# Perceiver layer, cross-attention units: the mix of high and low context parts in 512-column matmuls, the sum moved to the normalisation, and the row maximum ahead of the last low third

## The reference, cut to what matters

```
xn  = layernorm(ctx)                 # 2 x 1024 x 256
ln  = layernorm(layernorm(x))        # 2 x 64 x 256
q   = ln @ Wq ;  k, v = split(concat(xn, ln) @ Wkv)
sim = rmsnorm(q) * scale @ rmsnorm(k)^T      # per head, 1088 keys
attn = softmax(sim)
x  += (attn @ v) @ Wout + bout
```

## Time and profile before

| | us |
|---|---|
| median of 3 runs | 232.57 (232.32 to 232.83) |
| profiled execution, its own time | 233.34 |
| its span, first to last instruction | 231.4 |
| TensorE busy | 220.6 |
| VectorE busy | 152.0 |
| ScalarE busy | 154.9 |
| GpSimd busy | 80.2 |

### The profile page before, as it was taken

The page is one execution under the profiler, slowest core; times in us unless marked ns, Lnnn a source line. Parts: engine busy times, 40 slices in busy tenths (PEclk is TensorE's granted clock), DMA queues, the critical chain, the costliest instruction groups (busy, mean ns, idle before and its releaser), DMA issues.

```text
span 231.4 us, 4188 instructions
## 1 busy us (share of the span) xinstructions
PE 220.6 (95%) x1446; PEld 190.8 (82%) x1446; DVE 152.0 (66%) x347; ACT 154.9 (67%) x340; POOL 80.2 (35%) x131
## 2 busy tenths in 40 slices
PE   7899999999989999999999999999999998999884
PEld 6556778887778888989888989899999987899773
DVE  2699899998778786776866755566766661303431
ACT  2868777979885968776676567778787755314151
POOL 5188897861592837445160500000000010000300
PEclk9999999999999999999999999999999999999999
DMA  6590134200000000000000899700000000000000
GB/s 184 151 317 32 47 122 175 68 25 0 23 0 3 1 4 0 0 3 0 0 0 3 256 428 328 177 3 0 0 4 0 1 3 0 0 3 0 0 3 23
DMA packets 11252, 13.80 MB, mean 60 GB/s; under 512 B 1592, under 2 KB 9952, under 8 KB 10976
## 3 DMA queue, kind: packets, MB, share of 16 engines
q1 hardware_dynamic: 10680, 11.97, 16.6%
q10 hardware_dynamic: 552, 1.58, 1.9%
HBM read 13.15 MB, written 0.13 MB: 57 GB/s over the span
## 4 chain that ended last, share of the span: by engine, by line
PE 65%; DVE 21%; ACT 5%; issue 4%; DMA 2%; POOL 2%; ACTq 0%; POOLq 0%; DVEq 0%
PE banks L1307 19%; PE banks L1157 14%; PE banks L1216 8%; PE banks L1248 8%; PE banks L1447 5%; DVE small L902 4%; DVE sk L914 4%; PE banks L1321 3%; DMA wraw<-in_L_xattn_Wkv 2%; PE banks L1250 2%; ACT knT L632 2%; PE banks L1370 2%; PE banks L1474 2%; DVE small L871 1%; DVE raw L865 1%
## 5 line engine op out<-in xcount | busy, mean ns | idle before, releaser
L937 DVE TENSOR_TENSOR ptl<-banks,pth 128x512 fp32r<-128x512 f32 (+1 forms) x48 | 26.8, 558 | 24.2 <-ACT pth L668 23.2
L1307 PE MATMUL banks<-xnh,pth 128*128 128x256 f32 x128 | 37.6, 294 | 0.1
L1307 PE MATMUL banks<-xnh,ptl 128*128 128x256 f32 x128 | 36.2, 283 | 0.0
L1307 PE MATMUL banks<-xnl,pth 128*128 128x256 f32 x128 | 36.2, 283 | 0.0
L515 POOL TENSOR_TENSOR small<-small 128x16 f32<-128x16 f32 x7 | 20.4, 2915 | 32.1 <-DVE small L909 32.1
L668 ACT ACTIVATE pth<-banks 128x512 fp32r<-128x512 f32 (+1 forms) x48 | 23.7, 495 | 10.6 <-PE banks L1157 9.5
L615 ACT ACTIVATE sk<-banks 128x512 f32<-128x512 f32 x36 | 20.7, 602 | 12.1 <-PE banks L1216 11.6
L902 DVE TENSOR_REDUCE small<-sk 128x8 f32<-128x512 f32 x36 | 23.6, 678 | 5.9 <-ACT sk L615 5.9
L914 DVE TENSOR_TENSOR sk<-banks,small 128x512 f32<-128x512 f32 x36 | 23.0, 680 | 6.6 <-POOL small L515 6.5
L495 POOL COPY sp<-sp 128x64 f32<-128x64 f32 x16 | 3.8, 238 | 62.8 <-ACT sp L649 62.7
L1157 PE MATMUL banks<-ident,sp 128*128 128x128 f32 x144 | 24.2, 279 | 1.1 <-ACT sp L649 1.1
(11 more groups left out here) (193 smaller groups left out, 478.0 us busy)
## 6 DMA issues: line engine op xcount, KB each, us to landing
knT<-in_L_attn_qkv_kernel SPq DMA_DIRECT2D x1, 3072.0 KB, 12.4
raw<-in_ctx SPq DMA_DIRECT2D x16, 128.0 KB, 2.3
knT<-in_L_xattn_Wq SPq DMA_DIRECT2D x1, 1024.0 KB, 6.8
wv<-in_L_xattn_Wkv ACTq DMA_DIRECT2D x1, 1024.0 KB, 4.9
wout_sb<-in_L_xattn_Wout SPq DMA_DIRECT2D x1, 1024.0 KB, 5.8
knT<-in_L_attn_out_kernel SPq DMA_DIRECT2D x1, 1024.0 KB, 15.2
wraw<-in_L_xattn_Wkv ACTq DMA_DIRECT2D x1, 512.0 KB, 5.0
wraw<-in_L_xattn_Wkv SPq DMA_DIRECT2D x1, 512.0 KB, 5.3
```

Of the source, the lines that this page charges most:

```text
L937: nc.vector.tensor_tensor(ptl[:, j0:j1, :], banks[:, t3_bank(u, c), 0:(j1 - j0) * P].rearrange("p (j r) -> p j r", j=j1 - j0), pth[:, j0:j ...
L1307: nc.tensor.matmul(banks[:, u_bank(u), 0:D], p_[:, j, :], x_, start=(j == 0 and i == 0), stop=False)
```

## The change

Units 8 to 14 become **wide** (`wide(u)`). `xnh` and `xnl` lie side by side in one array `xn2`, so that one matmul with 512 moving columns multiplies `pth` by both: high by high goes to the first half of the bank, high by low to the second. The matmul of `ptl` by `xnh` and those of the latents stay at 256 columns in the first half. The two halves are added where the mix is normalised: ScalarE scales the second half into `un` (`un_half`), then VectorE adds the first half, scaled, in one scalar_tensor_tensor (`mix_sum`), at the start of its work for the next unit.

The second half of the bank is now taken, so the transposed mix of a wide unit goes to the second half of bank 5 (`uT_bank`). That half holds the transposed feed-forward weights until L764 has copied them, so the wait for `w1T_ready` moves from ahead of the last logits third to ahead of `mix_transposed(u - 1)`.

From unit 7 on, `logits_max(u + 1)` is ahead of the low third `probs_low(u, 2)` on VectorE.

```diff
-        xnh = sb("xnh", [P, B * NT, D], F32R)
-        xnl = sb("xnl", [P, B * NT, D], F32R)
+        xn2 = sb("xn2", [P, B * NT, 2, D], F32R)
+        xnh = xn2[:, :, 0, :]
+        xnl = xn2[:, :, 1, :]
...
+        def wide(u):
+            return G <= u < UNITS - 1
+        def uT_bank(u):
+            return 5 if wide(u) else u_bank(u)
... (ScalarE, mix_out)
+                if wide(u):
+                    nc.scalar.activation(un[:, :], banks[:, u_bank(u), D:2 * D], ACT.Copy,
+                                         scale=rinv[:, u:u + 1]).then_inc(un_half, 1)
+                    return
... (ScalarE, mixT_out)
-                nc.scalar.activation(uT[:, :, :], banks[:, u_bank(u), D:2 * D].rearrange("p (c r) -> p c r", c=DC),
+                nc.scalar.activation(uT[:, :, :], banks[:, uT_bank(u), D:2 * D].rearrange("p (c r) -> p c r", c=DC),
... (VectorE)
+            def mix_sum(u):
+                dve.wait_ge(un_half, u - G + 1)
+                nc.vector.scalar_tensor_tensor(un[:, :], banks[:, u_bank(u), 0:D], rinv[:, u:u + 1], un[:, :], ALU.mult,
+                                               ALU.add).then_inc(un_ready, 1)
...
                 else:
+                    if wide(u - 1):
+                        mix_sum(u - 1)
                     probs_low(u, 0)
...
+                    if i + 1 >= ITEMS and u + 1 < UNITS:
+                        logits_max(u + 1)
                     probs_low(u, 2)
-                    if u + 1 < UNITS:
+                    if i + 1 < ITEMS:
                         logits_max(u + 1)
... (TensorE, mix)
+                        if wide(u):
+                            nc.tensor.matmul(banks[:, u_bank(u), :], pth[:, j, :],
+                                             xn2[:, b * NT + j, :, :].rearrange("p a d -> p (a d)"), start=(j == 0),
+                                             stop=False)
+                            nc.tensor.matmul(banks[:, u_bank(u), 0:D], ptl[:, j, :], xnh[:, b * NT + j, :], start=False,
+                                             stop=False)
+                            continue
... (TensorE, mix_transposed)
-                transposes(banks[:, u_bank(u), D:2 * D], lambda c: un[:, c * P:(c + 1) * P], DC).then_inc(ut_ps, 1)
+                transposes(banks[:, uT_bank(u), D:2 * D], lambda c: un[:, c * P:(c + 1) * P], DC).then_inc(ut_ps, 1)
... (TensorE, the loop over units)
                     if u >= G:
                         logits(u + 1, 0)
+                    if w1T_first < u <= w1T_first + len(w1T_blocks):
+                        pe.wait_ge(w1T_ready, u - w1T_first)
                     mix_transposed(u - 1)
...
                     probs_transposed(u, 2)
-                if w1T_first < u <= w1T_first + len(w1T_blocks):
-                    pe.wait_ge(w1T_ready, u - w1T_first)
                 logits(u + 1, 2)
                 mix(u)
```

More of the change, by code:

```diff
@@ L253, in perceiver_layer @@
         un_ready = sem("un_ready")
+        un_half = sem("un_half")
         ut_ps = sem("ut_ps")
```

## The result

The changed kernel takes 233.93 us (median of 6 runs, 233.60 to 234.08) against 232.53 for the kernel before (6 runs, 232.32 to 232.83). The ratio is 1.0055 with a 95% interval of 1.0042 to 1.0068: slower by 1.4 us, where 1.2 was forecast. The profiled execution took 233.99 us with a span of 232.2.

What follows compares the result with a forecast made beforehand. TensorE, busy for 95% of the span, was taken to bound the kernel. The terms 2.5 + 0.17 - 0.87 - 0.6 = +1.2 us, added to the 232.57 us median, gave 233.8 us, range 232.9 to 234.7.

Steps and rivals of the forecast that it cites:

- Part 3: Units 10 to 14: TensorE waits for ScalarE's weight copy before the mix transposes, 0.50 us each, a 2.5 us loss.
- Part 1: Starts of units 8 to 10: the earlier maximum closes TensorE's waits before the first transposes, a 0.87 us gain.
- Part 2: Wide units 8 to 14: 512-column matmuls save 10 ns in each of 56 context tiles, a 0.6 us gain.
- Part 4: Unit 9: TensorE waits 0.10 us for VectorE's added sum, 0.17 with refill, a loss of 0.2 us.
- refill: TensorE's queue restarting after a wait: four transposes take 0.42 us instead of 0.35, 0.07 us extra per wait.
- a weight load that idles 0.43 us on each copy: Units 10 to 14, sign of the forecast: the `un` transposes' weight load idles on L764's copy, some 2.1 us in all.
- the period: Sign of the forecast: the time per unit, 7.0 us before, rises to about 7.4.
- the copy cannot come earlier: ScalarE's weight copy hangs on TensorE's own transposes and the eviction between, so all of it shifts together.
- some 0.1 us of unit 10 would show: Claim that the weight copy's wait covers VectorE's sum in units 10 to 14; without it unit 10 would stall.
- TensorE makes up the wait: Rival, units 10 to 14: the 2.5 us vanish because TensorE is not truly the bound; 231.3 us, chance 0.08.
- the holes stay: Rival, units 8 to 10: ScalarE's `kh` copy holds the exponential equally long, losing the 0.87 gain; 234.6 us, chance 0.08.
- the wide matmuls gain nothing: Rival, units 8 to 14: 512-column matmuls gain 0.2 us or less instead of 0.6; 234.2 to 234.4, chance 0.2.

Runs made afterwards that it cites:

- the early wait alone: Kernel before, with only TensorE's wait for the weight copy moved ahead of mix_transposed(u - 1) in units 10 to 14: 234.97 us, ratio 1.0105.
- the maximum alone: Kernel before, with only logits_max(u+1) moved ahead of probs_low(u, 2) from unit 7 on: 231.68 us, ratio 0.9961.
- the own bank: Changed kernel, with the transposed mix back in the second half of its unit's bank and the weight-copy wait in its old place: 231.50 us.
- the matmuls split: Changed kernel, with each 512-column matmul made two of 256 columns into the two halves of the bank: 234.28 us.
- the copy first: Changed kernel, with ScalarE's weight copy ahead of the first high third's eviction (probs_high(u, 0)) in units 10 to 14: 231.39 us.
- unit 8 stays narrow: Changed kernel with the transposed mix in its unit's bank and the wait in its old place, but wide units only 9 to 14: 231.26 us.

## Why the prediction was right, step by step

The direction and the size came out as forecast: +1.4 measured, +1.2 forecast. The parts can be read in two ways. One is the difference of the medians. The other is the stretch of the profile that the change touches, from the start of unit 7's last mix matmul to the start of unit 14's: 139.09 to 187.38 = 48.29 us in the kernel before and 49.50 in the changed one, 50.73 with the early wait alone (138.31 to 189.04), 47.46 with the maximum alone (138.29 to 185.75), 47.19 with the own bank (138.43 to 185.62), 50.05 with the matmuls split.

| part | forecast, us | by medians, us | by the stretch, us |
|---|---|---|---|
| 3, the copy's wait | +2.5 | +2.48 (alone), +2.43 (taken out of the change) | +2.44 (alone), +2.31 (taken out) |
| 1, the maximum first | -0.87 | -0.81 (alone) | -0.83 (alone) |
| 2, 512 columns | -0.6 | -0.35 (split again) | -0.55 (split again) |
| 4, the sum | +0.2 | not run alone | +0.18 (0.12 of wait in unit 9 and a refill) |
| whole | +1.2 | +1.40 | +1.21 |

By the stretch every part (the copy's wait as run alone) lies within 0.06 us of its forecast, and the parts add up to +1.24 where the whole is +1.21. The remaining 0.2 us of the medians belongs to no part that the runs show. It is within what the times can tell, as the interval of the ratio means +1.0 to +1.6 us. The work ahead of the stretch varies by more from one execution to the next: the kernel before and the one with the early wait do the same there, and reached its start at 139.09 and at 138.31 us.

**Part 3** held to a few hundredths. What carried it was the coincidence in the earlier trace rows: the copy started just when TensorE reached `un`, so its whole length and the signal become a wait. The refill was 0.06 and not 0.07 us, in both places: in the nanosecond starts of the traces four transposes take 412 ns after a wait and 356 without, two take 274 and 216. The 0.07 came from the rounding of the rows. The sign named for it, a weight load that idles 0.43 us on each copy and 2.1 in all, did not appear as stated: the list of waits has 0.7 each and 3.5 in all, because the loads run ahead of their matmuls. The other sign, the period, did (7.46). The 2.31 of the own bank is lower because three more of its mixes (units 10, 12 and 14) have the slower of the two paces, some 0.04 us each. The statement that the copy cannot come earlier was true of the change as written, with ScalarE's order given. It is not true of the kernel: moved ahead of `pth` it starts 0.20 us after the probability transposes instead of 1.13.

**Part 1** held. The link named as late next, `kh` on ScalarE, is what the exponential now waits for. The sentence that from unit 11 on the move gives nothing missed a little: in unit 15, behind the stretch, the way from the first transposes to `un` takes 0.88 us in the changed kernel, where it was 0.91.

**Part 2** held in its sum, with some luck in the step that led there. The forecast took the spacing of the split logits (0.23, a saving of 10 ns per tile) over that of the key projections (0.237, 3 ns), because the logits lie in the same units. No unit saves 10 ns. Three save 7 and four save 13, and their mean in this execution is the 10 that was forecast. Only one execution of each kernel was profiled. With the own bank six of seven units have the slower pace and with the copy first only unit 8 has it, so the gain can lie anywhere from 0.4 to 0.7 us (an estimate: 56 tiles at 7 or at 13 ns), and the prediction gave no reason why it should be in the middle. The Trainium skill ("TensorE: Matmul & The Clock Gate", "Back-to-back issue gap") has a fixed 2.5 ns for each warm matmul, in a formula that it states for a single, isolated one. With 56 matmuls removed this would be 0.14 us, an estimate; the stretch shows 0.55, so the trace doesn't agree with it.

**Part 4** held for unit 9 and unit 15 (in the changed kernel TensorE's transposes there show no wait). One sentence in it was wrong: with the copy's wait gone, "some 0.1 us of unit 10 would show". In the run with the own bank TensorE's `un` transposes of unit 10 start at 152.69, 1.14 us after the probability transposes at 151.55, so without a hole. The weight transposes ahead of it give 0.22 us more, and the part's own numbers say so: 1.47 against 1.35.

**The rivals.** That TensorE makes up the wait was excluded by the early wait alone. That the holes stay was excluded by the maximum alone. That the wide matmuls gain nothing (0.2 or less) or run near the column rate (2.2) was excluded by the split run, with 0.35 by the medians and 0.55 by the stretch. The description of the change says that the second half of the bank "is now taken"; the own-bank run shows that it is free when the transposes come, so the move to bank 5, and with it the wait, wasn't needed.

## What to carry to other kernels

When a wait moves to an earlier place on the engine that bounds, look at the producer's queue, not at the distance of producer and consumer in the program: here the copy finished 0.43 us after the new waiting point in each of five units, and that was the loss. A producer with idle time ahead of it may take the step earlier for nothing; swapping two ScalarE instructions gave back 2.5 us. Before a result is moved to another bank, ask when its old place comes free: here the signal that is waited for anyway covered it. When a change touches one stretch of a kernel and is worth a few tenths of a microsecond, compare that stretch in the profiles and not the whole time alone: the part ahead of it varied by 0.8 us between executions here, while the four parts, read in the stretch, add up to the whole within 0.03 us.

## What was not expected of the hardware

**Two paces of the wide mix.** A tile of one matmul of 512 columns and one of 256 takes 0.353 us in some units and 0.347 in others, and one unit keeps its pace for the six tiles measured. The slower pace is in units 8, 11 and 13 of the changed kernel, in all wide units but unit 9 with the own bank, in unit 8 alone with the copy first, and in unit 9 alone when unit 8 stays narrow. Tiles of three matmuls of 256 columns take 0.360 in every unit from 8 to 14 of every run that has them. The instructions are the same in both cases, and no run shows what decides between the two.

**A copy on GpSimd beside VectorE.** GpSimd's small copy of the latents' probabilities took 0.24 us in every unit of the kernel before. In the changed kernel it took up to 0.32, where the earlier exponential makes it fall beside VectorE's `kl` subtraction, which reads two arrays from SBUF:

```profile
144.09 1.22 DVE L968 TENSOR_TENSOR kl<-knT,kh 128x1024 fp32r<-128x1024 f32 x1
...
145.09 0.32 POOL L507 COPY sp<-sp 128x64 f32<-128x64 f32 x1 [6.30 <-ACT sp L661]
```

The Trainium skill ("GPSIMD Engine Reference", "Specifications") says that GpSimd shares its SBUF interfaces with VectorE and contends with instructions that have two SBUF inputs; this case agrees, with 0.08 us, and nothing waited for it. The runs separate it in part. With the maximum first alone the copy falls beside `kl` in units 9 to 14 and takes 0.31 to 0.32 us there, and nothing else of the change is in that kernel. With the early wait alone it does not meet `kl` and takes 0.24 in every unit, in units 12 to 15 beside a reduction on VectorE that reads one array from SBUF. No run moves the copy alone.
